# Wide attention: the output products go behind the transposes of the probabilities, and the keys behind the queries

## The reference

```python
Q = queries @ Wq; K = keys @ Wk; V = values @ Wv      # 128 -> 16 heads x 64, times the masks
scores = einsum('bhqd,bhkd->bhqk', Q, K) / sqrt(64)
attn = softmax(scores) * ind_k; attn = attn / where(sum(attn) == 0, 1, sum(attn))
out = einsum('bhqk,bhkd->bhqd', attn, V)
x = x + out @ Wo
```

## Time and profile before

| | |
|---|---|
| time, median of 3 runs | 1573.92 us (1569.56 to 1578.9) |
| the profiled execution | 1575.54 us, of it the span 1573.7 us |
| TensorE matmuls | 1298.7 us busy, 83% |
| TensorE weight loads | 1111.4 us, 71% |
| VectorE | 1021.5 us, 65% |
| ScalarE | 938.6 us, 60% |
| GpSimd | 589.5 us, 37% |
| mean clock of TensorE | 0.927 of full speed |

### The profile page before, as it was taken

How to read it: one execution, slowest core, us unless ns; L and a number is a source line. 1 busy time by engine, 2 the same in 40 slices (tenths; PEclk the granted TensorE clock), 3 DMA queues, 4 the chain that set the end, 5 groups by cost and what they waited for, 6 DMA issues and landing times. The chain is left out here.

```text
span 1573.7 us, 42308 instructions
## 1 busy us (share of the span) xinstructions
PE 1298.7 (83%) x16531; PEld 1111.4 (71%) x16555; DVE 1021.5 (65%) x2551; ACT 938.6 (60%) x2128; POOL 589.5 (37%) x576
## 2 busy tenths in 40 slices
PE   7999999978999997994379874977743888888994
PEld 5898999856888895883146552976741777688994
DVE  7888997825443336996799978433326788763445
ACT  4766666623444456996446533654536989735884
POOL 3443333310000003432468731777750024443662
PEclk9999999999999999996689887999985999988997
DMA  9111100089991002320000010111122001002335
GB/s 325 51 31 33 30 19 3 3 115 154 150 147 2 1 1 76 111 85 1 14 15 19 12 55 8 50 48 48 50 89 76 16 24 38 30 32 58 96 92 180
DMA packets 140982, 93.81 MB, mean 60 GB/s; under 512 B 55456, under 2 KB 126752, under 8 KB 140272
## 3 DMA queue, kind: packets, MB, share of 16 engines
q1 hardware_dynamic: 131920, 72.79, 22.6%
q0 software_dynamic: 8864, 18.30, 3.6%
HBM read 51.06 MB, written 39.99 MB: 58 GB/s over the span
## 5 line engine op out<-in xcount | busy, mean ns | idle before, releaser
L438 POOL TENSOR_TENSOR wide_probs<-wide_probs,wide_key_mask 128x512 f32<-128x512 f32 x44 | 62.9, 1449 | 119.9 <-ACT wide_probs L620 119.9
L1717 POOL DMA_INDIRECT moe_x_rows<-moe_rows,moe_source x71 | 78.9, 1111 | 72.3 <-DVE moe_source L1816 51.0
L882 POOL MEMSET attn_v_bd<- 128x576 f32 x2 | 1.2, 615 | 265.9 <-POOLq L168 265.9
L912 POOL TENSOR_TENSOR attn_col_bd<-attn_col_t,group_mask_sb 128x1024 f32<-128x1024 f32 x32 | 60.6, 1894 | 100.0 <-ACT attn_row_t L1125 100.0
L2422 DVE TENSOR_TENSOR moe_hidden<-banks,moe_gate 128x256 f32<-128x256 f32 x103 | 43.2, 423 | 83.3 <-ACT moe_gate L2630 79.6
L3243 ACT ACTIVATE moe_router<-banks,moe_rb_sb 128x512 f32<-128x512 f32 x64 | 41.4, 688 | 91.6 <-PE banks L3347 66.4
L2087 POOL DMA_INDIRECT moe_rows<-moe_xhat,moe_slot x64 | 61.9, 967 | 68.7 <-DVE moe_slot L2387 49.7
L2259 POOL DMA_INDIRECT moe_results<-moe_y_rows,moe_x_rows x71 | 68.0, 958 | 51.2 <-issue 29.6
L1000 DVE TENSOR_REDUCE attn_top<-banks 128x32 f32<-128x2048 f32 x32 | 73.0, 2282 | 18.9 <-PE banks L1186 18.7
L1154 ACT ACTIVATE attn_probs<-attn_probs 128x1024 f32<-128x1024 f32 x64 | 65.8, 1053 | 25.7 <-DVE attn_probs L1029 24.2
L1723 POOL DMA_INDIRECT moe_results<-moe_y_rows,moe_dest x71 | 72.9, 1027 | 21.6 <-issue 21.0
(11 more groups left out here) (460 smaller groups left out, 4296.5 us busy)
## 6 DMA issues: line engine op xcount, KB each, us to landing
moe_rows<-route_empty_sb SPq DMA_DIRECT2D x8, 2624.0 KB, 25.1
attn_ctx<-in_ctx_t SPq DMA_DIRECT2D x48, 128.0 KB, 2.1
moe_x_rows<-moe_rows SPq DMA_DIRECT2D x71, 66.0 KB, 1.9
moe_pack_sb<-in_moe_pack SPq DMA_DIRECT2D x8, 578.0 KB, 3.9
moe_w_sb<-in_moe_w SPq DMA_DIRECT2D x2, 2048.0 KB, 10.5
moe_hot<-moe_results SPq DMA_DIRECT2D x16, 256.0 KB, 5.8
moe_until_back<-moe_results SPq DMA_DIRECT2D x16, 256.0 KB, 6.0
moe_pack_sb<-in_moe_pack SPq DMA_DIRECT2D x9, 384.0 KB, 4.7
```

The source lines that it names most:

```text
L438: nc.gpsimd.tensor_tensor(some, some, keys, ALU.mult).then_inc(masked, 1)
L912: nc.gpsimd.tensor_tensor(col_bd[:], col_t[u.parity][:].unsqueeze(1).to_broadcast(shape), w["group_mask"][:].unsqueeze(2).to_broadcast(sha ...
L1717: nc.gpsimd.indirect_dma_start(x_rows[s % GATHERS][:], None, rows, bass.IndirectOffsetOnAxis(ap=source[:, s:s + 1], axis=0)).then_inc(gath ...
```

## The change

In each step TensorE's output products of item d, with their waits, stand directly behind the second half of the transposes of e, ahead of the queries of p. So the keys of p stand directly behind the queries. No instruction is added or taken away, no buffer or semaphore is changed, and the lists of the other four engines are the same.

```diff
--- before.py
+++ after.py
@@ -706,6 +706,17 @@
                     if inside(e):
                         pe.wait_ge(pt_taken, 2 * e + 1)
                         turn(e, 1)
+                    if inside(d):
+                        arrived(core, pe, "wide_later")
+                        pe.wait_ge(ht_taken, 2 * d + 2)
+                        if d % GROUP == 0 and d >= GROUP:
+                            pe.wait_ge(added, d // GROUP)
+                        for t in range(GROUP):
+                            for f in range(2):
+                                ins = nc.tensor.matmul(y_bank[:, t * P:(t + 1) * P], heads_t[:, 2 * t + f],
+                                                       w["wide_wo"][:, 2 * (d % GROUP) + f], start=(d % GROUP == 0 and f == 0 and t == 0),
+                                                       stop=(d % GROUP == GROUP - 1 and f == 1 and t == GROUP - 1))
+                        ins.then_inc(made_y, 1)
                     if inside(p):
                         pe.wait_ge(high_taken, p // GROUP + 1)
                         pe.wait_ge(low_taken, p // GROUP + 1)
@@ -717,17 +728,6 @@
                             if p == 0 and n == 0:
                                 pe.wait_ge(split_low, 1)
                             project(p_bank[n], 2 * (p % GROUP) + n, wq_high, wq_low, x_high[:], x_low[:], q_made)
-                    if inside(d):
-                        arrived(core, pe, "wide_later")
-                        pe.wait_ge(ht_taken, 2 * d + 2)
-                        if d % GROUP == 0 and d >= GROUP:
-                            pe.wait_ge(added, d // GROUP)
-                        for t in range(GROUP):
-                            for f in range(2):
-                                ins = nc.tensor.matmul(y_bank[:, t * P:(t + 1) * P], heads_t[:, 2 * t + f],
-                                                       w["wide_wo"][:, 2 * (d % GROUP) + f], start=(d % GROUP == 0 and f == 0 and t == 0),
-                                                       stop=(d % GROUP == GROUP - 1 and f == 1 and t == GROUP - 1))
-                        ins.then_inc(made_y, 1)
                     if inside(p):
                         g = p // GROUP
                         pe.wait_ge(ctx_high_ready, g + 1)
```

## The result

The changed kernel takes **1602.48 us** (median of 4 runs, 1592.99 to 1606.15) against 1576.13 for the kernel before (4 runs, 1569.56 to 1578.9) on the same chip: ratio 1.0146 [1.0114, 1.0178]. It is slower by 23 us (18 to 28), where 8.3 was forecast; the range ended at 1588.5. The profiled execution took 1606.15 us, with a span of 1604.3 and a mean granted clock of 0.928 (before: 1575.54, 1573.7, 0.927).

The account below looks back on a forecast made before the run. TensorE's instruction stream was taken to bound the wide attention: 27 steps at +0.30 us gave 8.1, plus 0.2 for a VectorE instruction in step 15, 8.3 on the median 1573.92, so 1582.2 us; range 1576.5 to 1588.5.

Parts of the forecast that it names:

- the keys' hole: Keys wait for the query copy and start 0.46 to 0.47 behind the last query matmul instead of 0.23.
- the block sum of 5.40: Second transposes to head products, summed as 3.62 + 1.78 = 5.40 us against 5.10 before: +0.30 a step over 27 steps.
- the next stage follows the last step: Everything behind the wide attention stays as long as it was; its last head products come about 8.3 us later.
- the 3.62: Transposes to head products in step 5, without output products, keys right behind queries: 3.62 us, said to include both keys' waits.
- L461: VectorE's last scale-and-shift instruction in step 15 would meet the second GpSimd mask: +0.2 us taken, from -1.0 to +0.8.
- the case that I had priced at +0.8: In step 15, L461 is held by one more GpSimd instruction: +0.8 us.
- (a): Up to 3.5 us given back in TensorE's waits in step 16 and the tail: 4.8 slower, 1578.7 us; chance 0.20.
- (b): ScalarE late in six steps ahead of a group, TensorE waiting for probability copies: 11.9 slower, 1585.8 us; chance 0.15.
- (c): Fewer changes of matmul kind on TensorE save 0.10 in each of 27 steps: 2.7 faster, 1571.2 us; chance 0.05.
- The stated test for being wrong: Hole absent or 0.4 and more, a second entry in TensorE's waits between 46 and 300 us, or differences behind 325 us.

Follow-up runs that it names:

- outs_after_keys: Against the changed kernel, the whole group of output products moved to between the keys and the head products; ratio 1.0051 to the kernel before.
- split_2_2: Against the changed kernel, two of four token blocks of output products moved to between queries and keys; median 1581.73 us, ratio 1.001 to the kernel before.
- split_2_2_shift2: Half of the output products between queries and keys, as well as WARMING 26, putting block boundaries 32 records earlier; one run, 1660.90 us (kernel before there 1644.02).
- shift16: The changed kernel with 8 more warming matmuls (16 records) ahead of the stage, WARMING 18 instead of 10; one run, 1596.4 us.
- hold_late: The kernel before, order untouched, with the second keys half also waiting for the same step's normalization; ratio 1.0077 to the kernel before.

## Why the prediction was wrong

**Right, mostly to 0.01:** TensorE's stream is the time of the stage; the keys' hole and the block sum of 5.40; +0.31 a step and 8.3 us in all (outs_after_keys) against 0.30 and 8.1; nothing on ScalarE, VectorE and GpSimd became late; the next stage follows the last step.

**The step that failed** is the sentence on the second half of the keys: "What that costs is inside the 3.62, as step 5 has this wait too", and with it the sum, which priced the keys' waits only where they stand. Step 5's block was a true price of the hole. But it ended at the head products, so it could not hold a halt in the scores. I took early steps, behind which TensorE does not halt, as a measure for 27 steps, behind 11 of which it does. The move did two things: it took the cover from the copy (0.31 a step), and it took 1.5 us from the distance between the opening of that wait and the scores, 3.5 to 2.0. The second was worth 12.9 us and had no term.

It was to be seen. The page before has the line of q8 with 134 packets, that is one for some 250 records of the engine that bounds the stage, and I asked of no engine's queue but the data queues what the change does to it.

**L461:** +0.2 was forecast, with -1.0 to +0.8. In the changed kernel it takes 1.19 and ends at 145.25, with a mask of GpSimd that ends at 145.22, and the wait behind it is 1.07 instead of 1.2: nothing. In split_2_2 the case that I had priced at +0.8 came true (timeline, GpSimd and VectorE, step 15):

```profile
134.43 2.52 POOL L438 TENSOR_TENSOR wide_probs<-wide_probs,wide_key_mask 128x512 f32<-128x512 f32 x2 [6.24 <-ACT wide_probs L620]
...
136.03 0.95 DVE L458 TENSOR_TENSOR wide_query_scale<-rstd,mask_f_col_sb 128x16 f32<-128x16 f32 x1
136.90 1.28 POOL L430 TENSOR_TENSOR wide_ctx<-wide_ctx,wide_mask_row 128x512 f32<-128x512 f32 x1
137.02 1.20 DVE L461 SCALAR_TENSOR_TENSOR wide_query_shift<-mean,wide_query_scale 128x16 f32<-128x16 f32 x1
```

Two VectorE instructions of 16 columns, L458 and L461, each end with a GpSimd instruction (136.98 with the mask's 136.95, 138.22 with 138.18), and TensorE's wait grew to 1.95. The Trainium skill, SBUF — State Buffer, Who interferes with whom, says of that pair that a Vector instruction with two SBUF inputs contends with a GpSimd instruction that reads SBUF; this trace agrees. But TensorE's step 16 grew by 2.2, from 11.1 to 13.27, and the wait only by 0.7. The rest has another reason, which the granted clock shows (windows, split_2_2):

```profile
142.00:145.00 3.00, 3.00 (x13) 2.71 (x12) 1.46 (x2) 0.80 (x3) 0.00 (x0) 0.50 0.02 5
```

Right behind the wait of 1.95 us TensorE had 0.50, the 1.2 GHz level, for some 3 us, and the same in split_2_2_shift2 behind 1.94. Behind the waits of 1.23 (before) and 1.07 (after) at the same place it kept 1.00. The forecast had no term for that either.

**The rivals.** (a) came true in part: 1.4 of 3.5 are given back in the tail. VectorE's chain there did not follow TensorE's loss of 0.6 in step 33, and its normalization met the mask in the other order, which saved 0.8. The second is luck of the timing: in shift16 and hold_late, which halt as well, the wait is 2.3 as before. (b) did not happen: ScalarE's first probability copy of step 7 starts 4.29 behind the keys, as forecast (4.31), after an idle time of 0.20. (c) is ruled out: the steps without halts are 0.31 longer. The sign was right, at a chance of 0.53; no case reached 1602, since none held a loss that no semaphore shows. The stated test for being wrong ("a second entry between 46 and 300 us") is what happened.

## What to carry to other kernels

A wait on the bounding engine has two prices: how long the engine stands at it, and how close its opening lies to the next dense stretch of small instructions, since instructions are supplied in blocks, and in step 6 of six of the eight traces the next block was asked for only when it had opened. Before moving a block of long instructions away from between a wait and such a stretch, measure the distance from the wait's opening to the stretch in the trace (3.5 us was just safe here, with 3.0 a halt cost 0.2, with 2.0 to 2.4 it cost 0.3 to 1.5), and look for "issue" gaps that cut a row of equal matmuls in two. A block copied from another place in the same trace prices the waits in it, but not what the supply of instructions does behind it.

## What the runs showed of the hardware

- A halt on TensorE without any semaphore, 0.3 to 1.5 us of idle time, in matmuls and weight loads together, on a grid of 125.1 matmul records (after). With 16 records added ahead of the stage (shift16) nine of eleven halts stood on the same counts from the start of the program, up to 250 us later; two went and three came.
- From the start of an instruction packet to TensorE going on: 2.2 to 2.9 us over the eleven halts of the trace after. From the opening of the wait to the packet: 1.1 to 1.6 us there, and 1.3 in step 6 in both orders.
- The 128 records of 64x64 with their loads run in 2.04 us; a block lasts from 1.9 us there to 9.0 where the 128x512 matmuls are in it (trace before). All halts of over 0.2 us lay in the dense stretch or within 20 matmul records behind it.
- A satisfied wait isn't free: with hold_late no matmul stands at it in the 27 steps, and the kernel is 0.8% slower.
- Behind a wait of TensorE of 1.95 us the granted clock fell to 0.50 for some 3 us (split_2_2, step 16); behind 1.23 and 1.07 at the same place it did not. In the tail, behind a wait of 2.3 us, it fell to 0.50 in shift16 and hold_late and stayed at 1.00 in the kernel before.
